# A macaron block in float32 on one core: first block and both borders reordered, with multiplications of zeros while TensorE waits

## The reference, cut to what matters

```python
def ffn(x):                      # x: (2, 4096, 256), float32; W_*: 256 x 256
    x_prev = shift_right_by_one_row(x)            # zeros ahead of row 0
    xr = mu_r * x + (1 - mu_r) * x_prev
    xk = mu_k * x + (1 - mu_k) * x_prev
    return sigmoid(xr @ W_r.T) * (square(relu(xk @ W_k.T)) @ W_v.T)

def memory(x):
    k = (x @ Wk.T + bk) as 64 quaternions;  k = k / max(|k|, 1e-12)
    v = (x @ Wv.T + bv) as 64 quaternions
    mem = cumsum(quat_mul(v, k), axis=1)
    ret = quat_mul(mem, conj(k)) / sqrt(position)
    return x + (layernorm(ret) * ln_g + ln_b) @ Wo.T + bo

x = x + 0.5 * ffn(layernorm(x))
x = x + memory(layernorm(x))
x = x + 0.5 * ffn(layernorm(x))
```

## Time and profile before

| | us |
|---|---|
| median of 3 runs | 671.86 |
| lowest and highest | 669.58 and 672.56 |
| profiled execution, its own time | 670.52 |
| span of the profiled execution | 668.8 |
| PE busy | 619.1 (93%) |
| DVE busy | 561.3 (84%) |
| POOL busy | 545.2 (82%) |
| ACT busy | 429.2 (64%) |

### The profile page before, as it was taken

How to read it: one execution, slowest core, us unless ns; L and a number is a source line. 1 busy time by engine, 2 the same in 40 slices (tenths; PEclk the granted TensorE clock), 3 DMA queues, 4 the chain that set the end, 5 groups by cost and what they waited for, 6 DMA issues and landing times.

```text
span 668.8 us, 12336 instructions
## 1 busy us (share of the span) xinstructions
PE 619.1 (93%) x3412; PEld 524.6 (78%) x3412; DVE 561.3 (84%) x1170; ACT 429.2 (64%) x792; POOL 545.2 (82%) x626
## 2 busy tenths in 40 slices
PE   2899999999978999999999999999767999999997
PEld 2788988988856777777777777777546988998996
DVE  5889999997669999999999999999847877877773
ACT  4576776776456766666676666666354776776762
POOL 3498888887538999999999999999916788889864
PEclk9999999999998999999999999999877999999999
DMA  8730000000000000000000000000000101101111
GB/s 247 236 116 1 0 0 0 0 0 1 1 0 1 0 2 0 0 0 0 0 0 0 0 0 0 0 0 1 0 1 0 65 32 63 63 31 63 63 63 65
DMA packets 19257, 18.66 MB, mean 28 GB/s; under 512 B 1312, under 2 KB 19232, under 8 KB 19232
## 3 DMA queue, kind: packets, MB, share of 16 engines
q1 hardware_dynamic: 19232, 18.36, 8.7%
HBM read 9.97 MB, written 8.39 MB: 27 GB/s over the span
## 4 chain that ended last, share of the span: by engine, by line
PE 79%; DVE 6%; POOL 5%; ACT 5%; issue 4%; DMA 1%; POOLq 0%; DVEq 0%; ACTq 0%
PE bank L1088 25%; PE bank L1119 17%; PE bank L1177 15%; PE bank L1223 7%; PE bank L1102 4%; PE bank L1204 3%; PE bank L1197 3%; ACT m_xnT L822 2%; PE bank L1171 2%; PE bank L1179 2%; DVE diff L404 1%; POOL rhalf L281 1%; POOL bhalf L261 1%; POOL rhalf L282 1%; POOL bhalf L262 1%
## 5 line engine op out<-in xcount | busy, mean ns | idle before, releaser
L1177 PE MATMUL bank<-wkv,m_xnT 128*128 128x256 f32 x512 | 132.7, 389 | 11.4 <-ACT m_xnT L822 11.4
L1119 PE MATMUL bank<-wffn,kact 128*128 128x256 f32 x512 | 118.8, 386 | 6.8 <-DVE kact L420 6.8
L1177 PEld LDWEIGHTS bank<-wkv,m_xnT 128*128 128x128 f32 x512 | 90.5, 192 | 34.9 <-ACT m_xnT L822 18.5
L1119 PEld LDWEIGHTS bank<-wffn,kact 128*128 128x128 f32 x512 | 96.8, 194 | 19.7 <-issue 7.2
L295 POOL TENSOR_TENSOR xk_lo<-xk,xk_hi 128x1024 fp32r<-128x1024 f32 x30 | 71.1, 2369 | 35.1 <-ACT xk_hi L736 35.1
L992 POOL TENSOR_TENSOR xr_lo<-xr,xr_hi 128x1024 fp32r<-128x1024 f32 x32 | 76.3, 2385 | 14.2 <-ACT xr_hi L742 12.6
L999 POOL TENSOR_TENSOR res<-res,gating_buffers 128x1024 f32 (+1 forms) x31 | 74.8, 2413 | 15.5 <-DVE gating_buffers L427 14.2
L585 DVE TENSOR_TENSOR xn<-bank,khat 128x1024 f32<-128x1024 f32 x64 | 77.7, 1216 | 2.1
L585 DVE TENSOR_TENSOR gating_buffers<-bank,khat 128x1024 f32<-128x1024 f32 x64 | 77.5, 1210 | 0.0
L1088 PE MATMUL bank<-wffn_hi,xr_hi 128*128 128x256 f32 x256 | 72.0, 281 | 0.0
L1088 PE MATMUL bank<-wffn_hi,xr_lo 128*128 128x256 f32 x256 | 71.9, 281 | 0.0
(11 more groups left out here) (127 smaller groups left out, 1595.1 us busy)
## 6 DMA issues: line engine op xcount, KB each, us to landing
res<-x SPq DMA_DIRECT2D x16, 512.0 KB, 4.2
out<-res SPq DMA_DIRECT2D x15, 512.0 KB, 2.9
out<-res SPq DMA_DIRECT2D x2, 256.0 KB, 2.2
wffn<-w_k SPq DMA_DIRECT2D x1, 256.0 KB, 3.9
wffn<-w_r SPq DMA_DIRECT2D x1, 256.0 KB, 4.2
wffn<-w_v SPq DMA_DIRECT2D x1, 256.0 KB, 5.5
wo<-w_o SPq DMA_DIRECT2D x1, 256.0 KB, 6.8
wkv<-w_kv SPq DMA_DIRECT2D x1, 256.0 KB, 6.2
```

What stands on the lines that cost most here:

```text
L1119: last = nc.tensor.matmul(dst[:, i, :], x[:, f, i * P:(i + 1) * P], wffn[:, w, f, :], start=f == 0, stop=f == FC - 1)
L1177: nc.tensor.matmul(dst[:, i, :], m_xnT[:, f, i * P:(i + 1) * P], wkv[:, f, col:col + D], start=f == 0, stop=False)
```

## The change

`keep_warm(out_ap, n)` is new: n matmuls of the float32 tile `zeros` (128x256) with `upto` as weights, written where nobody reads. It is called in five places. SP loads the output weights ahead of the feed-forward weights, with a semaphore of their own for the small columns. The scaled and centred output weights get a tile of their own, `wo_centred`, and the preparation of the memory stage moves to the front of DVE's list. In the first body of a feed-forward stage the squares move up and `stats_of(1, 1)` moves behind both `mix_receptance`. The borders are reordered on all four engines.

```diff
             load_x(0, 0)
-            sp.dma_start(cols[:, :], columns).then_inc(consts_in, 16)
+            sp.dma_start(cols[:, :], columns).then_inc(cols_in, 16)
+            sp.dma_start(wo[:, :, :], w_o.rearrange("(f p) n -> p f n", p=P)).then_inc(wo_in, 16)
             for i, w in enumerate((w_k, w_r, w_v)):
                 sp.dma_start(wffn[:, i, :, :], w.rearrange("(f p) n -> p f n", p=P)).then_inc(consts_in, 16)
             load_x(1, 0)
-            sp.dma_start(wo[:, :, :], w_o.rearrange("(f p) n -> p f n", p=P)).then_inc(wo_in, 16)
...
+            def scale_output_weights():
+                dve.wait_ge(cols_in, 16)
+                dve.wait_ge(wo_in, 16)
                 for f in range(FC):
-                    nc.vector.tensor_scalar(wo[:, f, :], wo[:, f, :], lng[:, f:f + 1], None, ALU.mult).then_inc(wo_scaled, 1)
+                    nc.vector.tensor_scalar(wo_centred[:, f, :], wo[:, f, :], lng[:, f:f + 1], None, ALU.mult).then_inc(wo_scaled, 1)
+                dve.wait_ge(consts_pool, 1)
                 nc.vector.tensor_scalar(eps_pos[:, :], pos[:, :], LN_EPS, None, ALU.mult)
...
-                def first_mix(mixed_key, mixed_half, mixed):
+                def first_mix(mixed_key, key_split, mixed):
                     difference(0, 0)
                     mix_key(0, 0, 0)
                     mix_key(0, 0, 1)
                     mixed_key()
-                    mix_receptance(0, 0, 0)
-                    mixed_half()
-                    mix_receptance(0, 0, 1)
+                    if stage == 0:
+                        mix_receptance(0, 0, 0)
+                        mix_receptance(0, 0, 1)
+                    key_low(dve, nc.vector, e, 0, 0)
+                    key_split()
+                    if stage == 1:
+                        mix_receptance(0, 0, 0)
+                        mix_receptance(0, 0, 1)
                     mixed()
-                    key_low(dve, nc.vector, e, 0, 0)
...
                             difference(nj, nb)
+                            if first:
+                                square(j, b, 0)
+                                square(j, b, 1)
                             mix_key(nj, nb, 0)
                             mix_key(nj, nb, 1)
-                        if first:
-                            stats_of(1, 1)
-                        square(j, b, 0)
-                        square(j, b, 1)
+                        if not first:
+                            square(j, b, 0)
+                            square(j, b, 1)
                         if mixing:
                             mix_receptance(nj, nb, 0)
                             mix_receptance(nj, nb, 1)
+                        if first:
+                            stats_of(1, 1)
...
-                def first_khat():
+                def first_inverse():
                     key_sum(0, 0)
                     key_inverse(0, 0)
-                    key_unit(0, 0)
-                def first_bind():
+                def first_bind(meanwhile):
+                    key_unit(0, 0)
                     bind(0, 0, 0)
                     bind(0, 0, 1)
+                    meanwhile()
                     key_sum(0, 1)
                     key_inverse(0, 1)
@@ DVE, body of mem @@
+                        if has(b, -1) and not has(b, -2):
+                            x_variance(2, NT - CT, NT)
+                        if has(b, -2) and not has(b, -3):
+                            x_scales(2, NT - CT, NT)
@@ DVE, its list @@
             stats_of(0, 0)
+            scale_output_weights()
+            prepare_memory()
             split_weights_high()
             split_weights_low(0, 1)
             stats_of(0, 1)
-            first_mix(prepare_memory, lambda: None, lambda: None)
+            first_mix(lambda: None, lambda: None, lambda: None)
...
             x_variance(1, CT, NT - CT)
-            first_khat()
+            first_inverse()
             last_gating()
-            first_bind()
-            x_scales(1, CT, NT - CT)
-            memory_stats(NJ - 1, 1)
-            x_variance(2, NT - CT, NT)
-            x_scales(2, NT - CT, NT)
+            def other_layernorms():
+                x_scales(1, CT, NT - CT)
+                memory_stats(NJ - 1, 1)
+            first_bind(other_layernorms)
...
             first_mix(last_moments, last_scales, lambda: store_x(NP - 1, 0))
+            stats_of(1, 0)
             store_x(NP - 1, 1)
-            stats_of(1, 0)
@@ ACT @@
                     normalize(1, 0)
                     keep_moments(NJ - 1, 1)
-                    x_std_of(1, NT - CT, NT)
-                    act.wait_ge(m["x_scales_done"], 3)
+                    act.wait_ge(m["x_scales_done"], 2)
@@ ACT, body of mem @@
+                        if has(b, -1) and not has(b, -2):
+                            x_std_of(1, NT - CT, NT)
+                        if has(b, -3) and not has(b, -4):
+                            act.wait_ge(m["x_scales_done"], 3)
@@ ACT, its list @@
             receptance_high(0, 0)
-            evict_xT(0, 1, True)
             act.wait_ge(bias_rows_ready, 1)
...
+            evict_xT(0, 1, True)
@@ POOL, body of ffn @@
+                        if stage == 0 and has(b, 1) and not has(b, 2):
+                            first_power()
                         if has(b, 1):
                             key_low(pool, nc.gpsimd, e, *at(j, b, 1))
                             receptance_low(*at(j, b, 1))
-                        if stage == 0 and has(b, 1) and not has(b, 2):
-                            first_power()
@@ PE @@
+            def keep_warm(out_ap, n):
+                for _ in range(n):
+                    nc.tensor.matmul(out_ap, upto[:, :], zeros[:, :], start=True, stop=True)
...
             pe.wait_ge(consts_pool, POOL_CONSTS)
+            keep_warm(v_flat[:, 3 * D:4 * D], 4)
+            fold_bias()
+            keep_warm(v_flat[:, 3 * D:4 * D], 4)
             transposes(0, 0)
-            fold_bias()
             bias_rows()
+            keep_warm(k_ps[:, 0, 0:D], 8)
             transposes(0, 1)
...
             transposes(0, 0)
             ret_transposes(NP - 1, 0)
+            keep_warm(k_ps[:, 0, 0:D], 2)
             output(NP - 1, 0)
+            keep_warm(k_ps[:, 0, 0:D], 4)
             def last_output():
                 ret_transposes(NP - 1, 1)
+                transposes(0, 1)
                 output(NP - 1, 1)
-                transposes(0, 1)
                 pe.wait_ge(rprod_done[1], MS)
```

More of the change, by code:

```diff
@@ L205, in macaron @@
         consts_in = sem("consts_in")
+        cols_in = sem("cols_in")
         wo_in = sem("wo_in")
@@ L1074, in bias_rows @@
                 for f in range(FC):
-                    nc.tensor.matmul(v_flat[:, 3 * D:4 * D], mean_of[:, :], wo[:, f, :], start=f == 0, stop=f == FC - 1)
+                    nc.tensor.matmul(v_flat[:, 3 * D:4 * D], mean_of[:, :], wo_centred[:, f, :], start=f == 0, stop=f == FC - 1)
                 pe.wait_ge(bias_lines_ready, 1)
```

13 lines of the change are left out of this document (7 added, 6 removed).

## The result

The changed kernel took 662.45 us (median; 662.07 to 664.51 in 4 runs) beside 670.72 for the kernel before: 0.988 of it, 95% interval 0.986 to 0.990. The profiled executions differ by the same amount, 662.22 against 670.52. It was predicted faster, at 660.8 in a range of 655.5 to 666: right in direction and mechanism, with a gain forecast a quarter too large (10.4 against 8.3 between the profiled executions).

A forecast was written before the change was run, and what follows sets the result against it. PE was taken to bound the kernel (79% of the span), so earlier entry into its unbroken stretches counts: 0.2 + 4.2 + 6.0 = 10.4 us off 670.52 gives 660.1, put at 660.8 for the median; range 655.5 to 666.

The forecast's parts named there:

- First block: Start of stage 0: key product of block 1 2.4 us earlier, less 2.2 for the clock, net +0.2 us.
- the term of the first zeros: Start of stage 0: zero matmuls cost PE 0.6 to 2.3 us, hidden up to about 1 us by DVE's statistics.
- the 2.2 taken: Each new wait ahead of block 1's key product: lower clock costs 2.2 us, bounds 0 and 3.0.
- Border to memory: Stage 0 to memory: keys of memory step 2 4.45 us earlier, less 0.25; 4.2 us, bounds 3.5 and 5.9.
- what is given back in the first steps: First memory steps: moved scales cost DVE 0.9 us where it leads; 0.25 taken, bounds 0 and 0.9.
- Border to stage 1: Memory to stage 1: key product of block 1 8.2 us earlier, less 2.2 for the clock, net 6.0 us.
- the signs that the prediction named: Both first bodies and memory: `value` near 24.5 and 500, key product near 33 and 508.7, over 4 us idle, keys near 197.
- The sum: Whole kernel: 0.2 + 4.2 + 6.0 = 10.4 us gained, from 670.52 to 660.1, put at 660.8.
- No clock cost: Rival, two new waits of both stages: the clock stays up, 14.8 us gained, about 656; chance 0.13.
- Low start: Rival, kernel start: clock stays low in the first zeros ahead of PE's real work; 662 to 666, chance 0.15.
- Given back by POOL: Rival, later feed-forward blocks: POOL bounds PE in every block, the earlier start is lost; 671, chance 0.07.
- slower: Rival, behind the two new gaps: long low clock outweighs the gain; 680 if each gap cost 25 us; chance 0.03.

The follow-up runs named there:

- b_inverse_later: Changed kernel with POOL's scale and shift of block 3 moved behind the low part of xk of block 1 in both first bodies: 654.43 us, 0.9748.
- c_fill_gaps: Changed kernel with 8 more zero matmuls behind the transposes that follow the first value product, in both feed-forward stages: 658.48 us, 0.9814.
- i_memory_border_alone: Kernel before with only the border from stage 0 to memory changed: 667.80 us, 0.9953.
- l_inverse_later_on_before: Kernel before with only POOL's scale and shift of block 3 moved behind the low part of xk of block 1: 670.82 us, 0.9992.
- e_low_early: b_inverse_later with DVE making the low part of W_r ahead of the low part of xk: 652.39 us, 0.9729.

## Why the prediction was right, step by step

**First block: +0.2 forecast, -0.2 measured.** The step that decides it, `stats_of(1, 1)` ahead of POOL's low part, is shown: 4.1 us from the end of the statistics (29.60 + 0.38 = 29.98) to the end of the low part (34.08), where 4.2 were forecast, and removing it gave 8 us over the two stages. `value` came at 26.06 instead of 24.5 and the key product at 34.13 instead of 33.1. The cause is the term of the first zeros. Their delay came out at its upper bound (transposes at 12.57, where 12.5 was worked out for the low clock), but the sum took it to be hidden behind DVE's statistics. The difference could begin only at 15.01 and not near 13. In b_inverse_later, where the same zeros were not late, the first key product started at 19.29 (20.27 here, 18.8 forecast). The statistics did not hide it, though they were late too: DVE's bias work had waited for PE's fold, so they ended at 13.8 and not at 12.75. That the lower level held for the second four zeros is read from their pace alone, since the granted clock that the profile prints for this stretch is 1.00:

```profile
10.00:12.00 2.00, 2.00 (x6) 1.63 (x5) 1.93 (x8) 0.21 (x1) 0.00 (x0) 1.00 1.05 320
```

The idle time ahead of the key product was 3.58 instead of 4.25 us, and its clock cost 1.3 us (7.09 us from key product to `value`, against 5.75 in c_fill_gaps), below the 2.2 taken and inside its bounds. So it is luck that the sum for this block is off by only 0.4 us: the product was 1.0 us later than forecast, and the clock cheaper by 0.9; another 0.3 goes because a product that starts out of a wait needs longer to `value` (5.75 us) than one behind its transposes (35.54 to 40.99 before).

**Border to memory: 4.2 forecast, 4.2 at the keys, 3.4 at the end of memory.** These are the gains up to there, 4.0 and 3.1, less the -0.2 of the first block. The times of `khat` (195.7 forecast, 196.25) and of the keys (197.1, 197.59) were met within 0.6 us. What I sized too small is what is given back in the first steps: 0.8, near the upper bound, where I took 0.25. The starts of the products with `after` show where: the lead over the kernel before is 3.74 us at 201.28, 3.58 at 212.43, 2.81 at 217.18, and 3.1 from 231 to the end of the stage. The timeline of DVE and PE in the changed kernel at the second of these steps down:

```profile
213.41 0.73 DVE L550 SCALAR_TENSOR_TENSOR x_shift<-x_moments,x_rstd 128x8 f32<-128x8 f32 x1
...
214.06 0.68 DVE L593 TENSOR_TENSOR khat<-bank,kinv 128x512 f32<-128x512 f32 x1
...
214.88 1.10 PE L1207 MATMUL bank<-wkv,m_xnT 128*128 128x256 f32 x4 [0.33 <-DVE khat L593]
```

The moved scales stand between `kinv` (212.29) and `khat`, which starts 1.77 us behind it; in the kernel before it is 0.98 (215.87 and 216.85). c_fill_gaps lost its lead at the same place. i_memory_border_alone, 3.2 us between the medians and 3.3 in the trace, agrees with the 3.4. The border held one thing that I had not foreseen: `x_gain`, a 128x8 operation, took 1.91 us, as the timeline of DVE and POOL in the changed kernel shows.

```profile
173.16 2.37 POOL L1017 TENSOR_TENSOR xr_lo<-xr,xr_hi 128x1024 fp32r<-128x1024 f32 x1
...
173.65 1.91 DVE L549 TENSOR_SCALAR x_gain<-x_rstd 128x8 f32<-128x8 f32 x1
```

It started half a microsecond after POOL's low part and ended with it, as the lock has it; the same operation takes 0.17 us elsewhere. So the scales came 1.7 us later than forecast. It cost little, since PE's key product ended at 177.1 anyway.

**Border to stage 1: 6.0 forecast, 5.2 measured (8.3 - 3.1).** On an axis moved by 3.1 us, the key product was forecast at 487.55 (487.55), `value` at 496.95 (497.14), the key product of block 1 at 505.6 (505.62). The whole of the difference lies behind this product: 8.59 us against the 5.65 of a later block, 2.94 us where 2.2 were taken, inside the bound of 3.0. c_fill_gaps, with 5.88, shows that 2.7 of them are the clock and not POOL. Of the signs that the prediction named, the idle time "over 4 us" ahead of both products was not reached (3.58 and 3.91); the others came, the two times in the first block 1.0 and 1.6 us late.

**The sum, 10.4 against 8.3.** The three shortfalls are 0.4, 0.9 and 0.8. Between the medians the gain is the same 8.3 us. The 0.7 us that I had added for the height of the median over the profiled execution (660.1 to 660.8) were hardly needed: the new median of the kernel before, 670.72, is close to the profiled 670.52.

**The rivals.** *No clock cost* did not happen; c_fill_gaps is this rival made true, at 658.5 and not 656, since the other shortfalls stay. *Low start* did in part: the second four zero matmuls ran for 3.76 us at the lower pace and pushed the transposes; the 662.45 measured also lies in the span given for it (662 to 666). *Given back by POOL* in later blocks and *slower* did not happen. The argument against *slower* took 6.8 us for the longest low stretch; by the pace of its matmuls, the start of the kernel before was low for longer (the first transposes, at 10.17, took 1.94 us, and the full pace came at 23.6). The 109 ns of the Trainium skill (TensorE: Matmul & The Clock Gate, section Back-to-back issue gap) do not hold for this float32 form in the changed kernel either: four zero matmuls (8 records) take 3.76 us at the lower clock, and eight (16 records) take 3.62 at the upper.

**What stays open.** Why the clock fell after 2.16 and 2.34 us of idle time in two kernels and not after 2.27 and 2.33 in two others. I had bounded the danger by the length of the wait alone, and the runs refute that. The plainest pair is `value` of block 0 of stage 0 in l_inverse_later_on_before and in i_memory_border_alone, whose edits touch nothing that PE waits for up to there:

```profile
30.85 3.69 PE L1121 MATMUL bank<-wffn,kact 128*128 128x256 f32 x16 [2.80 <-DVE kact L420]
...
30.38 5.38 PE L1128 MATMUL bank<-wffn,kact 128*128 128x256 f32 x16 [2.80 <-DVE kact L420]
```

The same wait left the clock up in the first (1.00 over 28 to 35) and not in the second (0.67 over 30.4 to 35.6). Open with it is why the first zeros ran at one pace in some executions and at the other in the rest.

**A better version.** e_low_early takes 652.39 us, 0.9729 of the kernel before and 10 us below the changed kernel.

## What to carry to other kernels

When a stall is taken off an engine, read at once what the next instruction behind it waits for and which lists that passes through: here an edit worth 8 us lay in one line of POOL's list, and was worth nothing in the kernel before the change. Cost a new wait of TensorE with the clock that it may lower, and do not take a short wait to be safe. Multiplications that keep the clock up belong into waits that are known to be longer than they are; in front of the first real work they cost here about what they gave. Before comparing two orders, look in both traces whether everything ahead of the edit ran at the same pace.

## What the runs showed of the hardware that I had not expected

DVE and POOL block each other over SBUF for whole instructions, decided by a tenth of a microsecond: 0.68 us against 2.86 to 2.89 for one subtraction (in four executions), 0.17 against 1.91 us for an operation on 8 columns. A kernel can win or lose 2.2 us at this place by the pace of TensorE some 8 us earlier, and comparing two orders needs it moved out of the way. And the clock fell after single idle times between 2.16 and 4.99 us, behind two of 1.59 and 0.72 us in one execution and not in another, stayed up after 2.27, 2.33 and once after 2.80, and cost 1.3 to 3.0 us in the stretches read here.
